# Norm statistics partly on VectorE, and a new order of work on every engine, in a two-block cross-attention kernel

## The reference, cut to what matters

```python
# block L0, 16 heads of 16
q, k, v = split(layernorm(x, ln1) @ w_qkv + b_qkv)
x = x + merge(softmax(q k^T / 4 * m1 - 10000 * (1 - m1)) v) @ w_ao + b_ao
q = layernorm(x, ln2) @ w_q + b_q
k, v = split(ctx @ w_kv + b_kv)
x = x + merge(softmax(q k^T / 4 * m2 - 10000 * (1 - m2)) v) @ w_co + b_co
x = x + gelu(layernorm(x, ln3) @ w1 + b1) @ w2 + b2
# block L1: queries from x, keys and values from the context and x together
q, k, v = x @ q_w + q_b, split(concat(ctx, x) @ kv_w + kv_b)
y = merge(softmax(where(mask, q k^T / 16, -inf)) v) @ out_w + out_b + x
out = gelu(rmsnorm(y) * postnorm_w @ mlp_w1 + mlp_b1) @ mlp_w2 + mlp_b2 + x
```

## Time and profile before

| what | value |
|---|---|
| median of 3 runs | 1072.71 us (1070.87 to 1075.0) |
| profiled execution, its own time | 1074.24 us |
| its span | 1072.0 us |
| TensorE busy, whole span | 1002.5 us (94%) |
| weight loads busy | 892.1 us (83%) |
| VectorE busy | 949.5 us (89%) |
| ScalarE busy | 859.3 us (80%) |
| GpSimd busy | 671.7 us (63%) |
| mean granted TensorE clock | 0.978 |

### The profile page before, as it was taken

One profiled execution on the slowest core, in us unless ns is written; L12 is line 12 of the kernel. 1 busy time (PEld: TensorE's weight loads), 2 busy tenths in 40 slices (PEclk: granted clock), 3 DMA queues, 4 the chain that ended last, 5 costly groups with the idle time before them and its releaser, 6 DMA issues.

```text
span 1072.0 us, 46440 instructions
## 1 busy us (share of the span) xinstructions
PE 1002.5 (94%) x19180; PEld 892.1 (83%) x19180; DVE 949.5 (89%) x2008; ACT 859.3 (80%) x1967; POOL 671.7 (63%) x1037
## 2 busy tenths in 40 slices
PE   5777989999999999999999999999999999998988
PEld 5666878888888888888888888888888888887877
DVE  4887988999999999999999999999999999987763
ACT  3447689888888888888889888888888888787995
POOL 3787577666667666666666666666666666755320
PEclk9787999999999999999999999999999999999999
DMA  8652221223322222232222222222222222321111
GB/s 297 208 161 78 46 47 37 50 55 59 49 49 47 54 51 52 55 60 54 50 48 53 54 45 58 56 59 49 50 46 55 50 54 44 67 47 37 32 22 41
DMA packets 169699, 67.70 MB, mean 63 GB/s; under 512 B 151184, under 2 KB 167312, under 8 KB 168464
## 3 DMA queue, kind: packets, MB, share of 16 engines
q1 hardware_dynamic: 169488, 64.72, 26.8%
HBM read 26.93 MB, written 4.19 MB: 29 GB/s over the span
## 4 chain that ended last, share of the span: by engine, by line
PE 30%; ACT 23%; DVE 18%; issue 11%; DMA 11%; SPq 5%; POOL 2%; ACTq 0%; POOLq 0%; DVEq 0%
PE psum L457 9%; ACT staging L2007 7%; PE psum L598 7%; ACT hid_mlp L2007 6%; PE psum L630 5%; DMA turned_cross<-pair_cross 4%; PE psum L470 4%; DMA heads_turned_cross<-heads_pair_cross 3%; ACT L1993 3%; DVE mx_lat L1239 3%; PE psum L564 2%; SPq L2779 2%; ACT parts_mlp L2016 2%; ACT probT_self L1993 1%; SPq L2761 1%
## 5 line engine op out<-in xcount | busy, mean ns | idle before, releaser
L2513 POOL TENSOR_TENSOR late<-late,mx_ctx 128x512 f32<-128x512 f32 x64 | 67.7, 1057 | 103.9 <-DVE mx_ctx L1245 103.9
L2507 POOL TENSOR_TENSOR prob_cross<-prob_cross,add_cross 128x512 f32<-128x512 f32 x64 | 91.1, 1441 | 57.5 <-DVE prob_cross L1229 57.4
L2507 POOL TENSOR_TENSOR prob_self<-prob_self,add_self 128x512 f32<-128x512 f32 x64 | 81.9, 1282 | 38.5 <-DVE prob_self L1229 32.3
L2007 ACT ACTIVATE hid_mlp<-psum,folded,undo_in 128x128 f32<-128x128 f32 x256 | 96.2, 458 | 7.8 <-PE psum L457 7.1
L2007 ACT ACTIVATE staging<-psum,cols,undo_in 128x128 f32<-128x128 f32 x256 | 97.8, 484 | 2.8 <-PE psum L457 2.3
L630 PE MATMUL psum<-hi_m,parts_mlp 128*128 128x256 f16 x512 | 95.3, 275 | 0.3 <-DVE parts_mlp L1288 0.3
L630 PE MATMUL psum<-hi_n,staging 128*128 128x256 f16 x512 | 93.9, 273 | 1.4 <-DVE staging L1288 1.4
L457 PE MATMUL psum<-turned_mlp,hi_m 128*128 128x128 f16 x1024 | 92.3, 219 | 3.1 <-DMA turned_mlp<-pair_mlp 1.4
L457 PE MATMUL psum<-turned_mlp,hi_n 128*128 128x128 f16 x1024 | 90.4, 220 | 0.8 <-DMA turned_mlp<-pair_mlp 0.3
L2484 POOL TENSOR_TENSOR xb<-x,rows 128x256 f32<-128x256 f32 x96 | 82.8, 873 | 10.2 <-DVE x L1298 5.7
L457 PE MATMUL psum<-turned_mlp,lo_m 128*128 128x128 f16 x512 | 88.7, 219 | 0.0
(11 more groups left out here) (262 smaller groups left out, 3766.4 us busy)
## 6 DMA issues: line engine op xcount, KB each, us to landing
xin<-in_x SPq DMA_DIRECT2D x32, 128.0 KB, 2.1
late<-in_ctxT SPq DMA_DIRECT2D x4, 1024.0 KB, 6.0
ctxT<-in_ctxT SPq DMA_DIRECT2D x32, 128.0 KB
late<-in_x SPq DMA_DIRECT2D x4, 1024.0 KB, 5.1
out<-xb SPq DMA_DIRECT2D x32, 128.0 KB, 2.0
staging<-in_w_m SPq DMA_DIRECT2D x2, 1024.0 KB, 7.1
staging<-in_w_n SPq DMA_DIRECT2D x2, 1024.0 KB, 5.0
mask<-in_mask_cross SPq DMA_DIRECT2D x32, 32.0 KB
```

The source lines that it names most:

```text
L2007: last = e.activation(hid[t][g][:, j * P:(j + 1) * P], ps[:, j * P:(j + 1) * P], ACT.Gelu_apprx_tanh, bias=b1[:, 4 * g + j:4 * g + j + 1], ...
L2507: e.tensor_tensor(ch, ch, over_heads(a[:, :]), ALU.add).then_inc(sem["added_" + t], 1)
L2513: e.tensor_tensor(ch, ch, over_keys(max_of("ctx", h)), ALU.subtract).then_inc(sem["shifted_ctx"], 1)
```

## The change

The change has two parts.

1. For the three layernorms, VectorE now also computes -mean and (variance + epsilon) * scale, each as an instruction on 128 x 1, right behind bn_aggr. `root` on GpSimd keeps the power and makes the shift as -mean * rstd, so it has two instructions where it had three. The rmsnorm (mlp1) keeps its own on GpSimd.
2. All five lists are written anew: the order in the start, the loop and the end, the lags of several stages, and the PSUM banks. The loop has 24 turns as before, with the same stages once in each turn.

In TensorE's loop `project(t - 3, "self")` becomes `project(t - 2, "self")` and moves from place 3 of the turn to its end, and the two `prob_turn` of ctx and lat move from the turn's start to its end (t - 6 becomes t - 5).

```diff
             def moments(u, t):
 
-                src, steps, n = residual(t, u), sem["moments_" + t], 2 * u
-                q.wait_ge("moments_" + t, n)
+                src, shrink = residual(t, u), 2.0 ** (-2 * XHAT_UP)
+                steps, n = sem["moments_" + t], 4 * u
...
                 e.bn_stats(bn[t][:, :], src[:, :]).then_inc(steps, 1)
                 q.wait_ge("moments_" + t, n + 1)
-                q.wait_ge("rstd_" + t, 3 * u)
                 e.bn_aggr(mv[t][:, :], bn[t][:, :]).then_inc(steps, 1)
+                q.wait_ge("moments_" + t, n + 2)
+                q.wait_ge("rstd_" + t, 2 * u)
+                e.tensor_scalar(minus_mean[t][:, :], mv[t][:, 0:1], -1.0, None, ALU.mult).then_inc(steps, 1)
+                e.tensor_scalar(var[t][:, :], mv[t][:, 1:2], L0_EPS, shrink, ALU.add, ALU.mult).then_inc(steps, 1)
...
             def root(u, t):
                 q.wait_ge("constants", MINUS_HALF)
-                shrink, done = 2.0 ** (-2 * XHAT_UP), sem["rstd_" + t]
                 if t == "mlp1":
                     q.wait_ge("mean_square_mlp1", u + 1)
-                    q.wait_ge("x_lo_mlp1", u)
-                    n, src, eps = 2 * u, mean_square[:, :], L1_EPS
+                    e.tensor_scalar(var[t][:, :], mean_square[:, :], L1_EPS, 2.0 ** (-2 * XHAT_UP), ALU.add,
+                                    op1=ALU.mult).then_inc(sem["rstd_mlp1"], 1)
+                    q.wait_ge("rstd_mlp1", 2 * u + 1)
                 else:
-                    q.wait_ge("moments_" + t, 2 * u + 2)
-                    q.wait_ge("xn_" + t, u)
-                    n, src, eps = 3 * u, mv[t][:, 1:2], L0_EPS
-                e.tensor_scalar(var[t][:, :], src, eps, shrink, ALU.add, op1=ALU.mult).then_inc(done, 1)
-                q.wait_ge("rstd_" + t, n + 1)
-                e.tensor_tensor(rstd[t][:, :], var[t][:, :], minus_half[:, :], ALU.pow).then_inc(done, 1)
+                    q.wait_ge("moments_" + t, 4 * u + 4)
+                q.wait_ge("x_lo_mlp1" if t == "mlp1" else "xn_" + t, u)
+                e.tensor_tensor(rstd[t][:, :], var[t][:, :], minus_half[:, :], ALU.pow).then_inc(sem["rstd_" + t], 1)
                 if t != "mlp1":
-                    q.wait_ge("rstd_" + t, n + 2)
-                    e.tensor_scalar(shift[t][:, :], mv[t][:, 0:1], rstd[t][:, 0:1], -1.0, ALU.mult, op1=ALU.mult).then_inc(done, 1)
+                    q.wait_ge("rstd_" + t, 2 * u + 1)
+                    e.tensor_tensor(shift[t][:, :], minus_mean[t][:, :], rstd[t][:, :], ALU.mult).then_inc(sem["rstd_" + t], 1)
...
             load_weight(0, "qkv")
+            load_columns(0)
             load_x(0)
-            load_columns(0)
```

More of the change, by code:

```diff
@@ L704, in _ @@
+            prob_turn_bank(3, "self", 5)
+            project(2, "self", 6)
+            v_ctx(0, 7)
+            k_cross(2, 4)
+            prob_turn(3, "self", 2)
             through(0, "lo", 7)
[L705 to L708, removed]
             score_bank(4, "self", 2)
[L710 to L713, removed]
@@ L774, in _ @@
[L774 to L788 removed]
+            score(4, "self", 5)
@@ new lines, in _ @@
+            hidden(0, "mlp0", 0, 7)
+            mix(3, "self", 3)
+            v_self(4, 1)
+            prob_turn(1, "cross", 7)
+            hidden(0, "mlp0", 1, 5)
+            mix(1, "cross", 0)
+            squared_weight(0, "n2", 4)
+            q_cross(2, 7)
+            prob_turn_bank(4, "self", 5)
+            qk_self(5, 2)
+            score_bank(2, "cross", 0)
+            score(2, "cross", 6)
+            prob_turn(4, "self", 4)
+            project(1, "cross", 3)
+            outward(0, "mlp0", 0, 1)
@@ new lines, in _ @@
+            score_bank(0, "ctx", 4)
+            score(0, "ctx", 6)
+            outward(1, "mlp0", 0, 3)
+            score_bank(0, "lat", 0)
+            score(0, "lat", 4)
+            v_lat(0, 2)
+            outward(1, "mlp0", 1, 3)
+            q_cross(3, 6)
+            k_ctx(1, 1)
+            score_bank(3, "cross", 2)
+            score(3, "cross", 6)
+            project(2, "cross", 5)
+            project(4, "self", 0)
+            prob_turn_bank(0, "lat", 7)
+            prob_turn_bank(0, "ctx", 5)
@@ L866, in _ @@
[L866 to L876 removed]
+            score_bank(2, "ctx", 1)
+            k_lat(2, 4)
@@ new lines, in _ @@
+            v_lat(2, 0)
+            v_ctx(2, 3)
+            prob_turn_bank(4, "cross", 6)
+            score(2, "ctx", 4)
+            mix(5, "self", 7)
+            outward(3, "mlp0", 0, 2)
+            k_ctx(3, 5)
+            prob_turn(4, "cross", 3)
+            outward(3, "mlp0", 1, 2)
+            score_bank(2, "lat", 0)
+            score(2, "lat", 6)
+            hidden(0, "mlp1", 1, 4)
+            mix(4, "cross", 3)
+            v_cross(5, 5)
+            v_self(6, 2)
+            qk_self(6, 4)
@@ new lines, in _ @@
+            score(UNITS - 3, "lat", 1)
+            outward(UNITS - 2, "mlp0", 0, 7)
+            prob_turn(UNITS - 1, "cross", 0)
+            outward(UNITS - 2, "mlp0", 1, 7)
+            mix(UNITS - 1, "cross", 6)
+            outward(UNITS - 6, "mlp1", 0, 3)
+            v_lat(UNITS - 3, 6)
+            hidden(UNITS - 5, "mlp1", 0, 0)
+            project(UNITS - 4, "lat", 5)
+            outward(UNITS - 6, "mlp1", 1, 3)
+            project(UNITS - 1, "cross", 4)
+            prob_turn_bank(UNITS - 3, "ctx", 0)
@@ L1684, in _ @@
[L1684 to L1695 removed]
+            heads_low(UNITS - 3, "cross")
```

1778 lines of the change are left out of this document (862 added, 916 removed).

## The result

The change makes the kernel slower: 1084.22 us median of four runs (1084.13 to 1085.23), beside 1072.82 for the kernel before, a ratio on record of 1.0103 with a 95% interval of 1.0073 to 1.0133 (the two medians alone give 1.0106). The forecast was 1067, on the faster side; its wide range of 1055 to 1085 still holds the measured time. The profiled execution took 1085.23 us with a span of 1083.3.

The account below looks back on a forecast made before the run. VectorE was taken to bound the changed kernel, with a 30.20 us turn. Profiled 1074.24 - 5.3 (loop) - 0.3 (start) = 1068.6, median 1.5 lower, so 1067; forecast's own range 1061 to 1068, 8-in-10 range 1055 to 1085.

Parts of the forecast that it names:

- The statistics: The norms' added VectorE instructions cost 0.27 us a norm, 0.81 a turn for three; bounds 0.6 to 1.6 a turn.
- what it saves is hidden: GpSimd, busy 132 of 200 us, loses one small instruction a norm; no gain in time was counted for it.
- The queue: SyncE's load_rest behind the transposing DMAs: TensorE's 0.81 us wait goes, but VectorE allows only 0.22 a turn, 5.3 us.
- Ahead of them stand a store and one load of x instead, which wait for nothing recent: In SyncE's queue, what now precedes turned_cross and turned_mlp in place of the four loads of load_rest.
- VectorE is now the bound: VectorE's turn without waits rises from 29.39 to 30.20 us, above TensorE's 29.15, and limits what the rest can give.
- rival A: No change: TensorE waits on VectorE's thirteen instructions between score(cross) and prob_turn(cross), taking back 0.22 us a turn; 1072.4 us, chance 0.31.
- I count this as zero: VectorE's collisions with GpSimd, 0.5 us apiece, counted as no net change; bounds -1.0 to +1.0 us a turn.
- TensorE's turn without waits: Before the change, a 30.42 us turn less 0.81 for a DMA wait and 0.46 for the exponentials: about 29.15 us.
- rival C: Much faster: collisions fall by 1.0 us a turn, TensorE bounds at some 29.5, 22 us less, 1050 us; chance 0.08.
- The prediction's rule for who collides: VectorE instructions with two SBUF inputs contend with GpSimd instructions that read SBUF; those with a single input do not.
- The wait for the exponentials: TensorE's wait for ScalarE's exponentials of self stays, at 0.46 us a turn, affordable in a turn of 30.2.
- B: Slower: VectorE's low_pair(cross) waits for GpSimd's later high_pair(cross), at least 0.2 us; with 0.8, 1086 us; chance with kin 0.27.

Follow-up runs that it names:

- s6_old_stats: Changed kernel with the store issued earlier and the statistics of the kernel before (GpSimd does all three small instructions): 1090.16 us, ratio 1.0147 to the kernel before.
- s1_store: Changed kernel with SyncE's store moved behind load_rest and one unit later, so issued about 15 us earlier: 1074.65 us, ratio 1.0000 to the kernel before.
- c1_small_add: Changed kernel with the earlier store; GpSimd adds the mask of cross to only 64 of 512 columns, computation incomplete: 1058.58 us, ratio 0.9869 to the kernel before.
- s2_chain: Changed kernel with VectorE's second largest_score(ctx) and low_pair(self) moved behind both shifted(cross): 1082.4 us, ratio 1.0082 to the kernel before.
- s3_store_chain: Changed kernel with the earlier store, and largest_score(ctx) and low_pair(self) behind both shifted(cross) on VectorE: 1068.01 us, ratio 0.9931 to the kernel before.
- s4_cast: Changed kernel with GpSimd's high_pair(cross) moved ahead of the root of mlp0: 1090.41 us, ratio 1.0144 to the kernel before.
- s9_table: Changed kernel with earlier store, largest_score(ctx) later and first shifted(self) earlier, plus an unused gelu ahead of ScalarE's q_bias_cross: 1059.61 us, ratio 0.9872 to the kernel before.

## Why the prediction was wrong

The statistics were sized well. L1171 takes 0.154 and L1172 0.144 us, and from bn_aggr to the next instruction that is not of the norm VectorE needs 0.35 us (560.02 to 560.37) where it needed 0.09: 0.26 a norm, 0.27 predicted. The words "what it saves is hidden", said of GpSimd's shorter root, do not hold in the new order: two roots stand ahead of the cast there, and `s6_old_stats` puts the saving at 15 us.

The queue was right as far as TensorE goes: no wait for a turned tile is left. The sentence "Ahead of them stand a store and one load of x instead, which wait for nothing recent" is the first step that failed. It asked what the store waits for, and not who waits for the store. `plus_bias(self)` had moved from unit t - 2 to t - 1, and with it the buffer had to be free one turn sooner. The store of that buffer is issued at the head of the next list, behind both `heads_across`. GpSimd's in-order queue carried this wait to the second norm. Its cost is the difference between 1.0103 and 1.0000: 7 us in the loop, 4 around it.

The second step that failed is "VectorE is now the bound", with a turn of 30.20. The ordinary turn is 30.67, and VectorE's need did not rise to 30.20: in `s1_store` it waits 20.7 us in 300 to 900, 1.06 a turn, which leaves 29.6. Its busy share fell to 94.0%, which the prediction had named as the sign that waits and not work set the turn. The mechanism of rival A was there in every turn, and its price was too small: 0.22 was assumed, 1.2 us of TensorE are lost. The count of instructions (thirteen against eight) was right; it was not turned into time with collisions in it. VectorE's side is 9.1 us, TensorE's cover 8.1. In the profiled executions the forecast was 1068.6 and 1085.2 was measured: 24 turns of 30.67 instead of 30.20 are 11 us of this, the long turns 7, and the start and the end, counted as -0.3, gave about 2 back.

"I count this as zero" for the collisions is the third. Their sum fell, by about 0.8 us a turn: `heads_low(lat)` went from 0.95 to 0.41 us, the low half of mlp1 from 0.79 to 0.48, each `shifted(cross)` from 0.86 to 0.68, and smaller ones besides, while each `shifted(self)` rose from 0.88 to 1.32 (means of 300 to 900 us). That is why VectorE's need stayed near where it was (29.4 and 29.6), although the statistics were added. But those that grew are on the loop, and `c1_small_add` shows them to be worth 0.67 us a turn. One number for the sum could not hold both.

TensorE's turn without waits, put at 29.15, was too short: it takes off 0.81 for a transposing DMA in every turn, while the two rows list 7.7 us in 16 waits of 19.7 turns. In `s1_store`, with these waits gone, 30.67 less the 1.2 for `prob_turn(cross)` leaves 29.5. The sum itself did not use it; the step that made VectorE the bound and rival C did.

The prediction's rule for who collides leaves out a condition. The Trainium skill ("SBUF — State Buffer", Who interferes with whom) says that a VectorE instruction with at most one SBUF input stays clear of GpSimd outside VectorE's two-port modes, and names tensor_scalar among those that can enter them. The rows decide here: the new tensor_scalar of the norms (L1171, L1172) took 143 to 155 ns throughout 300 to 900 us, and `masked(cross)`, with one SBUF input and right beside GpSimd's addition, 0.68 to 0.69 us.

The wait for the exponentials, kept at 0.46, is gone from the list; in the order of the turn TensorE comes to it behind the late `prob_turn(cross)`, and in `s2_chain` and `s3_store_chain`, where that wait nearly goes, it is back (2.7 and 3.0 us).

Of the rivals, B had the nearest time (1086, a turn near 31) and the right symptom, VectorE idle ahead of `pair_cross` behind GpSimd's cast in each turn. Its mechanism, the cast behind the root of mlp0, is real: it is the 0.30 us of every ordinary turn, where B said at least 0.2. But VectorE waits for `score(cross)` afterwards all the same (0.45), so the loop can absorb it. That is argued; `s4_cast` shows only that with the cast ahead the kernel is slower. What made the wait long, and B's number nearly right, was the store, so that nearness is luck. A alone is `s1_store`. It has the new wait that A names and nearly A's time (1072.4), but not A's turn of 30.42: the chain takes back more than the DMA waits gave (30.67), and only the shorter start, which A counted as 0.3, brings the time to that of before.

What stays open: why the store lands late in about every third turn. From its issue it takes 1.9 us in the median and up to 3.9, and in `s1_store` 2.2 and up to 4.2. It was only moved out of the way, and no run varied what is in flight beside it.

## What to carry to other kernels

When a list moves a stage to an earlier unit, follow its buffer to the store that frees it, and ask who stands behind the waiting instruction on that engine: the price comes out there and not where the wait is. When an engine is nearly full, find the closed loop between it and its neighbour and add up the loop in time, with each collision on it at its full length; an instruction off the loop is free to collide. Equal times don't mean that nothing changed: compare start, loop and end by themselves. Where two limits stand at the same height, they may hide each other, so a fix that gains nothing is not yet shown to be useless.

## What the runs showed of the hardware

- A subtraction of VectorE on 128x512 takes 0.68 us alone and up to 1.76 beside GpSimd's addition of the same size. Of GpSimd's two additions to cross in a turn, the one that stands before the subtractions takes 1.27 us and the one beside them 1.71. Both sides lose.
- The same small arithmetic (scale and epsilon on 128x1) occupies 0.144 us on VectorE and 0.19 to 0.52 on GpSimd, by its place in the kernel before, and in a dependent sequence on GpSimd it takes 0.27 with what lies between (433.61 to 433.88 in `s1_store`).
- A 128 KB store takes 1.9 us from issue to landing in the median and 3.9 at most, in the same place of the program (the changed kernel).
- A gelu on 128x1 ahead of a wait takes the loading of the table (1.28 us) with it, and ScalarE then starts its first gelu as soon as the product is there.
- Once no irregular DMA wait is left, most of the loop's turns repeat to 0.02 us (30.67, 30.26, 30.00 in three kernels); single ones are up to 0.15 longer.
- A weight-load share of 89% was no room: in `s9_table` the weight loads are busy 177.88 of 200 us, while the listed waits of TensorE are 0.19 us in a turn of 29.97.
